# Row mean from eight more columns of a weight matrix, in place of products with a constant matrix

## The reference

```python
# layer "L2" in the names: language_ids picks a matrix per batch b
h = relu(einsum('bsh,bha->bsa', x, W1[ids]) + b1[ids])        # 256 features -> 64
adapted = einsum('bsa,bah->bsh', h, W2[ids]) + b2[ids]        # 64 -> 256
z = x + adapted
mean = jnp.mean(z, axis=-1, keepdims=True)
var = jnp.mean(jnp.square(z - mean), axis=-1, keepdims=True)
x = x + (z - mean) * rsqrt(var + 1e-5) * gamma + beta
# layer "L3"
x = x + einsum('bnh,boh->bno', x, W[subject]) + bias[subject]
```

## Time and profile before

| | |
|---|---|
| median of 3 runs | 1583.36 (1583.22 to 1584.35) |
| the profiled execution | 1581.01, span of its instructions 1579.2 |
| TensorE busy | 1570.2 of 1579.2 |
| VectorE, ScalarE, GpSimd busy | 1133.2, 931.4, 671.3 |
| granted TensorE clock | 0.9 or more of full speed in all 40 slices of the page |
| chain that ended last | TensorE 93%, GpSimd 3%, issue 2% |

### The profile page before, as it was taken

One profiled execution on the slowest core, in us unless ns is written; L12 is line 12 of the kernel. 1 busy time (PEld: TensorE's weight loads), 2 busy tenths in 40 slices (PEclk: granted clock), 3 DMA queues, 4 the chain that ended last, 5 costly groups with the idle time before them and its releaser, 6 DMA issues.

```text
span 1579.2 us, 22425 instructions
## 1 busy us (share of the span) xinstructions
PE 1570.2 (99%) x7916; PEld 1339.7 (85%) x7916; DVE 1133.2 (72%) x1685; ACT 931.4 (59%) x1683; POOL 671.3 (43%) x621
## 2 busy tenths in 40 slices
PE   9999999999999999999999999999999999999999
PEld 7888888999988888888888888888888888888898
DVE  6855556788889876777777776776776777657567
ACT  6655555666666665565666566656666666555444
POOL 7865544766787431432432442342342352038000
PEclk9999999999999999999999999999999999999999
DMA  4111105555520000010010010010010010022000
GB/s 161 56 53 54 54 27 179 169 183 177 171 83 31 20 34 27 14 41 27 15 40 28 14 41 27 14 40 28 14 41 27 14 41 27 15 59 77 14 14 28
DMA packets 31012, 85.98 MB, mean 54 GB/s; under 512 B 5030, under 2 KB 10534, under 8 KB 30774
## 3 DMA queue, kind: packets, MB, share of 16 engines
q1 hardware_dynamic: 30310, 83.21, 16.0%
q0 software_dynamic: 304, 1.10, 0.2%
q10 hardware_dynamic: 288, 0.26, 0.1%
HBM read 82.46 MB, written 2.10 MB: 54 GB/s over the span
## 4 chain that ended last, share of the span: by engine, by line
PE 93%; POOL 3%; issue 2%; DMA 0%; ACT 0%; DVE 0%; SPq 0%; POOLq 0%; ACTq 0%; DVEq 0%
PE up L682 13%; PE up L684 13%; PE up L683 13%; PE sum L441 12%; PE sum L442 12%; PE sum L443 12%; PE up L441 4%; PE up L442 3%; PE up L443 3%; PE up L450 2%; PE up L449 2%; PE up L451 2%; POOL expert_in L1496 1%; DMA raw<-in_shared 0%; POOL shared_up L1496 0%
## 5 line engine op out<-in xcount | busy, mean ns | idle before, releaser
L1305 ACT ACTIVATE hidden_hi<-up_tile 128x512 fp32r<-128x512 f32 x256 | 161.1, 629 | 189.2 <-DVE up_tile L2125 166.7
L2130 DVE TENSOR_TENSOR hidden_lo<-up_tile,hidden_hi 128x512 fp32r<-128x512 f32 x256 | 197.9, 792 | 44.7 <-ACT hidden_hi L1305 44.7
L2120 DVE TENSOR_TENSOR gate_tile<-up,gate_tile 128x512 f32<-128x512 f32 x192 | 130.1, 687 | 137.7 <-PE up L684 137.5
L441 PE MATMUL sum<-hidden_hi,down 128*128 128x512 f32 x512 | 199.2, 389 | 0.0
L443 PE MATMUL sum<-hidden_hi,down 128*128 128x512 f32 x512 | 199.2, 389 | 0.0
L442 PE MATMUL sum<-hidden_lo,down 128*128 128x512 f32 x512 | 199.2, 389 | 0.0
L683 PE MATMUL up<-x_sums,gate_up 128*128 128x512 f32 x512 | 199.2, 389 | 0.0
L682 PE MATMUL up<-x_sums,gate_up 128*128 128x512 f32 x512 | 199.2, 389 | 0.0
L684 PE MATMUL up<-x_sums,gate_up 128*128 128x512 f32 x512 | 199.2, 389 | 0.0
L2125 DVE TENSOR_TENSOR up_tile<-up_tile,gate_tile 128x512 f32<-128x512 f32 x192 | 184.0, 985 | 2.2
L1298 ACT ACTIVATE gate_tile<-gate_tile 128x512 f32<-128x512 f32 x192 | 119.9, 633 | 90.4 <-DVE gate_tile L2120 88.1
(11 more groups left out here) (332 smaller groups left out, 4004.9 us busy)
## 6 DMA issues: line engine op xcount, KB each, us to landing
raw<-in_experts SPq DMA_DIRECT2D x64, 512.0 KB, 3.3
raw<-in_l SPq DMA_DIRECT2D x51, 512.0 KB, 3.3
raw<-in_shared SPq DMA_DIRECT2D x23, 512.0 KB, 3.3
raw<-in_w SPq DMA_DIRECT2D x8, 256.0 KB, 2.6
x<-in_xT SPq DMA_DIRECT2D x3, 512.0 KB, 9.2
l_stage<-in_l SPq DMA_DIRECT2D x3, 512.0 KB, 4.2
out<-out_stage SPq DMA_DIRECT2D x6, 256.0 KB, 2.2
gate_w<-in_gw POOLq DMA_DIRECT2D x1, 1024.0 KB, 7.0
```

What stands on the lines that cost most here:

```text
L441: pe.matmul(out, wh, vh, start=start, stop=False)
L1305: A(hi[:, i], cu[:, i], ACT.Copy).then_inc(hi_done, 1)
L2120: V.tensor_tensor(t, ps, t, ALU.add).then_inc(c_done[m], 1)
L2130: V.tensor_tensor(lo[:, i], cu[:, i], hi[:, i].bitcast(f32), ALU.subtract).then_inc(lo_done, 1)
```

## The change

`minus_mean`, `x_row_sum` and its parts, `mean_stage`, `mean_part`, `row_sum` and `row_sum_hi` are dropped, and with them the stages `xs` and `mean`. The first matrix `l2_w1` becomes `w1m` with 72 columns for each batch and half: columns 64 to 71 hold -1/256 in the high part and 0 in the low part. So rows 64 to 71 of the first product are the negative row mean. A second tensor `v` goes into the second of the two `down` products: its rows 0 to 63 are the rounded ReLU (a third ReLU), rows 64 to 71 the mean rounded (a copy of 8 rows on ScalarE), rows 96 to 103 the rest of the mean (a subtraction of 8 rows on VectorE), and the others zero, written once after step 10. The matching rows of `w2[b][:, 1]`, in which the low part of the second matrix uses only rows 0 to 63 now, hold 1 in rows 64 and 96 and 0 elsewhere (`pick`, copied by ScalarE for each batch). `res` adds `x` itself. The fills of the eight columns stand in `center_b2` where that of `minus_mean` stood, and `l2_up_stage` of unit 0 waits for `b2_done`. The numbers in `WHEN` of the stages that stay are the same.

```diff
-STAGES = ["x2", "xs", "up", "mean", "within", "hid", "down", "res", "square", "scale", "var", "eps", "diag", "rstd",
+STAGES = ["x2", "up", "within", "hid", "down", "res", "square", "scale", "var", "eps", "diag", "rstd",
           "norm", "add", "x3", "x3l", "l3a", "outa", "l3b", "outb"]
...
+    w1m = place("l2_w1_mean", [P, B, 2, DT, A2 + MEAN_ROWS], f32r, over="shared_sums", skip=11264)
...
+    v = place("l2_mean_hidden", [2 * A2, BLK], f32r, over="raw", skip=12288)
...
                 pe.wait_ge(w_lo, PLAIN0 + L1_CH * NE1 + b0 + nb)
                 if i == 0:
                     pe.wait_ge(small_full, 16 * late_small)
+                    pe.wait_ge(b2_done, 1)
...
                     for dt in range(DT):
-                        m = slice(dt * A2, (dt + 1) * A2)
                         if b == b0:
                             pe.wait_ge(x2_lo, DT * i + dt + 1)
-                        last = product(unit_ps[i][0:A2, 0, c], w1r[:, b, 0, m], w1r[:, b, 1, m],
+                        last = product(unit_ps[i][0:A2 + MEAN_ROWS, 0, c], w1m[:, b, 0, dt], w1m[:, b, 1, dt],
                                        xh[:, dt, t], xl[:, dt, t], dt == 0, dt == DT - 1)
                 last.then_inc(l2_up, 1)
 
-            def mean_part(i, m):
-
-                b0, nb, t0, c0, n = unit(i)
-                out = unit_ps[i][:, m, c0:c0 + n]
-                for dt in range(DT):
-                    for part in (xh, xl):
-                        pe.matmul(out, minus_mean[:], part[:, dt, t0:t0 + n], start=dt == 0 and part is xh, stop=False,
-                                  skip_group_check=True)
-
...
+            def l2_down_stage(i):
+
+                b0, nb, t0, c0, n = unit(i)
                 if i in (1, 2):
                     pe.wait_ge(out_ready, 2 * i)
-                if "xs" in WHEN[i]:
-                    pe.wait_ge(xs_lo, i)
-                    pe.matmul(out, minus_mean[:], xsr[i // 2][:, 0, 0:n], start=True, stop=False)
-                    pe.matmul(out, minus_mean[:], xsr[i // 2][:, 1, 0:n], start=False, stop=True).then_inc(mean_done, 1)
-                    return
-                last = product_of_parts(out, t0, n)
-                last.then_inc(mean_done, 1)
-
-            def product_of_parts(out, t0, n):
-
-                for dt in range(DT):
-                    pe.matmul(out, minus_mean[:], xh[:, dt, t0:t0 + n], start=dt == 0, stop=False)
-                    last = pe.matmul(out, minus_mean[:], xl[:, dt, t0:t0 + n], start=False, stop=dt == DT - 1)
-                return last
-
-            def l2_down_stage(i):
-
-                b0, nb, t0, c0, n = unit(i)
                 if i == END:
                     pe.wait_ge(out_ready, 6)
-                    mean_part(i, 1)
                     x_part(i, 0)
                 pe.wait_ge(hid_relu, i + 1)
-                if i == END:
-                    mean_part(i, 0)
-                else:
-                    pe.wait_ge(x_centered, i + 1)
                 pe.wait_ge(l2_hid, i + 1)
                 for b in range(b0, b0 + nb):
                     c = slice(b % 2 * S, (b % 2 + 1) * S)
                     for m in range(DT):
                         out, k = unit_ps[i][:, m, c], slice(m * P, (m + 1) * P)
-                        pe.matmul(out, w2[b][:, 0, k], u[:, c], start=i != END, stop=False, skip_group_check=True)
-                        last = pe.matmul(out, w2[b][:, 1, k], u[:, c], start=False, stop=True, skip_group_check=True)
+                        pe.matmul(out, w2[b][:, 0, k], u[:, c], start=True, stop=False)
+                        last = pe.matmul(out, w2[b][:, 1, k], v[:, c], start=False, stop=True)
...
                 A(w3[b][:, 0], raw[:, s, 0:512], ACT.Copy)
-                A(w1r[:, b, 0], raw[:, s, 512:640], ACT.Copy)
+                A(w1m[:, b, 0, :, 0:A2], raw[:, s, 512:640].rearrange("p (t m) -> p t m", t=DT), ACT.Copy)
                 act.wait_ge(w2_centered, b + 1)
+                A(w2[b][A2:2 * A2, 1], pick[A2:2 * A2].to_broadcast([A2, D]), ACT.Copy)
                 A(w2[b][:, 0], raw[:, s, 640:896], ACT.Copy).then_inc(w_hi, 1)
...
                 if i == 0:
                     act.wait_ge(w_lo, PLAIN0 + L1_CH * NE1 + B)
+                    act.wait_ge(mean_rows, 1)
                 act.wait_ge(l2_up, i + 1)
                 if i:
                     act.wait_ge(l2_down, i)
                     act.wait_ge(l2_hid, i)
                 for b in range(b0, b0 + nb):
                     c = slice(b % 2 * S, (b % 2 + 1) * S)
-                    A(ru[:, c], unit_ps[i][0:A2, 0, c], ACT.Relu, bias=b1[:, b:b + 1])
-                    last = A(u[0:A2, c], unit_ps[i][0:A2, 0, c], ACT.Relu, bias=b1[:, b:b + 1])
-                last.then_inc(hid_relu, 1)
-
+                    for out in (ru, u, v):
+                        A(out[0:A2, c], unit_ps[i][0:A2, 0, c], ACT.Relu, bias=b1[:, b:b + 1])
+                c, m = slice(c0, c0 + n), slice(A2, A2 + MEAN_ROWS)
+                A(v[m, c], unit_ps[i][m, 0, c], ACT.Copy).then_inc(hid_relu, 1)
...
-                lo_part(w1r[:, b, 1], raw[:, s, 512:640], w1r[:, b, 0])
-                lo_part(w2[b][:, 1], raw[:, s, 640:896], w2[b][:, 0]).then_inc(w_lo, 1)
-
+                lo_part(w1m[:, b, 1, :, 0:A2], raw[:, s, 512:640].rearrange("p (t m) -> p t m", t=DT), w1m[:, b, 0, :, 0:A2])
+                lo_part(w2[b][0:A2, 1], raw[0:A2, s, 640:896], w2[b][0:A2, 0]).then_inc(w_lo, 1)
...
+                if b == 0:
+                    dve.wait_ge(ident_full, 16)
+                    V.tensor_tensor(pick[:], ident[:, A2:A2 + 1], ident[:, A2 + 32:A2 + 33], ALU.add)
...
             def center_b2():
 
-                V.tensor_scalar(minus_mean[:], ones[:], -1.0 / D, None, ALU.mult)
+                same = ones[:].rearrange("p (b t m) -> p b t m", b=B, t=DT)
+                for h, value in enumerate((-1.0 / D, 0.0)):
+                    V.tensor_scalar(w1m[:, :, h, :, A2:A2 + MEAN_ROWS], same, value, None, ALU.mult)
                 dve.wait_ge(b2_sum, 1)
                 linked(V.tensor_reduce(b2s[:], unit_ps[0][:, 1, 0:DT * B].rearrange("p (b t) -> p b t", t=DT), AX.X, ALU.add))
                 V.scalar_tensor_tensor(b2c[:], b2s[:].rearrange("p (b t) -> p b t", t=1).to_broadcast([P, B, DT]),
                                        -1.0 / D, cols[:, :, 0:DT], ALU.mult, ALU.add).then_inc(b2_done, 1)
 
+            def zero_rows():
+
+                dve.wait_ge(w_lo, PLAIN0 + L1_CH * NE1 + B)
+                V.tensor_scalar(v[A2:2 * A2], ones[A2:2 * A2, 0:1].to_broadcast([A2, BLK]), 0.0, None, ALU.mult).then_inc(mean_rows, 1)
+
...
-                if i != END:
-                    dve.wait_ge(mean_done, i + 1)
-                    if i:
-                        dve.wait_ge(x3_done, DT * i)
-                    for dt in range(DT):
-                        last = V.tensor_tensor(y[:, dt, c], x[:, dt, t0:t0 + n], unit_ps[i][:, 1, c], ALU.add)
-                    last.then_inc(x_centered, 1)
                 dve.wait_ge(hid_relu, i + 1)
-                V.tensor_tensor(u[A2:2 * A2, c], ru[:, c], u[0:A2, c].bitcast(f32), ALU.subtract).then_inc(l2_hid, 1)
+                V.tensor_tensor(u[A2:2 * A2, c], ru[:, c], u[0:A2, c].bitcast(f32), ALU.subtract)
+                m, r = slice(A2, A2 + MEAN_ROWS), slice(A2 + 32, A2 + 32 + MEAN_ROWS)
+                V.tensor_tensor(v[r, c], unit_ps[i][m, 0, c], v[m, c].bitcast(f32), ALU.subtract).then_inc(l2_hid, 1)
 
             def res_stage(i):
 
                 b0, nb, t0, c0, n = unit(i)
                 dve.wait_ge(l2_down, i + 1)
-                if i == END:
-                    dve.wait_ge(x3_done, DT * 3)
-                else:
-                    dve.wait_ge(x_centered, i + 1)
+                if i:
+                    dve.wait_ge(x3_done, DT * min(i, SUMMED))
                 for dt in range(DT):
                     for b in range(b0, b0 + nb):
                         c = slice(b % 2 * S, (b % 2 + 1) * S)
-                        xc = x[:, dt, b * S:(b + 1) * S] if i == END else y[:, dt, c]
                         last = V.scalar_tensor_tensor(y[:, dt, c], unit_ps[i][:, dt, c], b2c[:, b, dt:dt + 1],
-                                                      xc, ALU.add, ALU.add)
+                                                      x[:, dt, b * S:(b + 1) * S], ALU.add, ALU.add)
                     last.then_inc(centered, 1)
...
             hooks.setdefault(9, []).append(center_b2)
+            hooks.setdefault(10, []).append(zero_rows)
```

More of the change, by code:

```diff
@@ L21 @@
 FT = F // P
+MEAN_ROWS = 8
 NB = 4
@@ L49 @@
 RING = [0, 1, 2, 0]
-STAGES = ["x2", "xs", "up", "mean", "within", "hid", "down", "res", "square", "scale", "var", "eps", "diag", "rstd",
+STAGES = ["x2", "up", "within", "hid", "down", "res", "square", "scale", "var", "eps", "diag", "rstd",
           "norm", "add", "x3", "x3l", "l3a", "outa", "l3b", "outb"]
 WHEN = [dict(zip(STAGES, at)) for at in (
[4 rows of a table removed]
-for u in (0, 3):
-    del WHEN[u]["xs"]
[4 rows of a table added]
```

(31 more changed lines are left out.)

14 lines of the change are left out of this document (2 added, 12 removed), and 8 rows, old and new, of the table WHEN.

## The result

| | before | after |
|---|---|---|
| median | 1583.29 (1581.06 to 1584.35, 6 runs) | 1593.88 (1591.81 to 1595.78, 6 runs) |
| ratio after to before | | 1.0069, 95% interval 1.0059 to 1.0079 |
| profiled execution, span | 1581.01, 1579.2 | 1593.19, 1591.4 |

The change costs 10.6 us, not 5.85, and the time lies above the range. The page of after, part 1, as the earlier trace rows: TensorE issues twenty products fewer, and the span is 12 longer.

The account below looks back on a forecast made before the run. TensorE, busy 99% of the span, was taken as the bound. Unit costs 2.65 + 0.1 + 2.05 + 1.05 = 5.85, added to the profiled 1581.01, plus 2.35 to the median, gave 1589.2; range 1584.8 to 1591.0.

Parts of the forecast that it names:

- The `pick` copies of the earlier batches cost nothing: Late weight preparation before unit 0: ScalarE's added copies fall in its idle time, cost zero.
- three signs of being wrong: 8-row copy well under 0.37, VectorE less than 1 us late at unit 3's `x_lo`, or TensorE idle under 2 us.
- The gain on TensorE: Last phase: dropped products free 3.3 us together; 48 products widened to 72 columns add 0.3.
- A narrow instruction isn't a cheap one here: Hidden rows of each unit: 8-row copy costs 0.57 and subtraction 0.68 for 512 columns, 0.36 and 0.42 for 256.
- The rival: Hidden rows: 8-row copy and subtraction take 0.15 each, giving 1585.5; chance 0.08, and 0.04 with every wait covered, 1580.7.
- The fills: Before unit 0's first matrix: two fills on VectorE, 0.68 pitch then 0.25; 0.5 more if GpSimd is later too.
- Unit 0's mechanism: TensorE waits for `b2_done`, then for hidden rows behind the 8-row subtraction, then for squares; unit 0 costs 2.65.
- Unit 1: Second matrix starts about as before, the TensorE gain being eaten; cost 0.1 (0 to 0.3).
- Units 2 and 3: ScalarE and VectorE 1.56 late from unit 2, lasting to unit 3's `x_lo`; cost 2.05 (1.3 to 2.5).
- that rival: Units 2 and 3: the lag is absorbed within unit 2, total cost 3.1, time 1586.5; chance 0.17.
- The last unit: Third ReLU, copy and second subtraction delay its second matrix, in series to the last store; cost 1.05 (0.8 to 1.3).
- The clock: TensorE's waits lower its clock: three microseconds at half clock cost 1.5 more, 1590.7; chance 0.05, shared with another late queue.

Follow-up runs that it names:

- before_pick: The kernel before with one ScalarE copy added in each of the eight late weight splits, overwritten by GpSimd afterwards: median 1583.9, ratio 0.9999.
- prep_alone: The kernel before plus the change's weight preparation alone (strided first matrix, pick copies, VectorE's addition), GpSimd's low part still on 128 rows: median 1584.1, ratio 1.0003.
- full_split: The changed kernel with GpSimd's low part of the second matrix on all 128 rows again, pick copies still issued but overwritten: median 1590.6, ratio 1.0047.
- no_pick: The changed kernel without ScalarE's eight pick copies and with GpSimd's low part on all 128 rows again: median 1590.4, ratio 1.0038.
- early_pick: The changed kernel with the eight pick copies moved to steps 1 and 2 and without VectorE's pick addition: median 1592.7, ratio 1.0056.
- reorder: The changed kernel with the eight mean rows copied and subtracted first, then two ReLUs per batch, the third ones last: median 1589.5, ratio 1.0032.
- polite: The changed kernel with GpSimd waiting, before a batch's three subtractions, until VectorE has centred the next batch's second matrix: median 1590.3, ratio 1.0048.
- all_polite: The changed kernel with pick copies and fills moved early, mean rows first, and GpSimd waiting for VectorE's centring: median 1587.0, ratio 1.0020.
- all_three: The changed kernel with pick copies in steps 1 and 2, fills in step 1, and mean rows copied and subtracted first: median 1587.7, ratio 1.0023.

## Why the prediction was wrong

The direction was right, and so were most steps. The one that failed:

**"The `pick` copies of the earlier batches cost nothing: ScalarE idles in each of those steps until VectorE's gate product comes."** Taken as a sentence on ScalarE's copies it held: before_pick and prep_alone are at 0.9999 and 1.0003. What I took from it, that steps 3 to 9 stay as they are, didn't. I never costed the edit next to it, GpSimd's low part on 64 rows in place of 128, since it takes work away. It made `x_lo` 2.4 late (predicted 0.31; the copies' own part is the difference of full_split and no_pick, 0.6), and full_split, which changes this alone, brings 1590.6, 6.4 above before with its unit 0 at 2.45, where I had 5.85 and 2.65. The chain runs: 64 rows shift VectorE by 0.4; the centring then falls just behind GpSimd's start, where it can take 2.6 (and does twice in after); the gate product, `hidden_hi` and the next batch's preparation come late; so do `x_hi` and `x_lo` of unit 0, and the last of GpSimd's work with them; TensorE waits 3.1 and not 1.5; the clock falls. Of the 2.9 between after and full_split in unit 0, 1.9 is the lag (2.4 less 0.5). The other 1.0 I put down to the clock; no run isolates it. The one with this lag, the same order of the hidden rows and no fall is early_pick, whose unit 0 costs 4.1 and not 5.3, which fits.

The bare trace of before had the warning: in the steps 3 to 9 VectorE's centrings took 757 ns in the mean, where a lone one takes 0.42, and one of them 1.49. That one began 0.07 behind GpSimd, where 2.60 came out in after. An operation whose duration varies threefold between steps here held a wait inside it. None of my three signs of being wrong came up (the 8-row copy took 0.59, unit 3's `x_lo` was over 1 late, TensorE idled for over 2): they looked at the units, and the miss lay in steps 3 to 9.

Step by step:
- *The gain on TensorE.* Right: the pitch of 72 columns is 0.12 (1461.99, 1462.11), the wide pace I had taken.
- *"A narrow instruction isn't a cheap one here."* Right: 0.59 and 0.69 for 8 rows where I had 0.57 and 0.68; 0.42 for 256 columns. The rival is out.
- *The fills.* Right: the first took 0.74 beside GpSimd's last subtraction, the second, begun at 1461.09 behind GpSimd's end at 1461.07, 0.21 (forecast a pitch of 0.68, then 0.25). GpSimd was later too, but so were the fills, and the 0.5 more that I had for that case didn't come.
- *The zeroing of `v`.* 0.42 and not 0.68; it was off the path.
- *ScalarE per batch.* The late weights take it 1.57 for each batch, 1.04 before: 0.53 more, not 0.31 (the pick copy has a pitch of 0.42, the strided copy of the first matrix costs 0.1 more than the plain one).
- *Unit 0's mechanism.* Confirmed where the lag is absent: first product behind `b_centered`, second matrix behind the 8-row subtraction, 2.2 to 2.45 against 2.65.
- *Unit 1.* 0.2 against 0.1. *Units 2 and 3.* 2.3 against 2.05; the lag isn't absorbed, that rival is out too. My sign for unit 3 (first matrix 1.5 late behind `x_lo`) showed as a wait of 0.4 there and longer ones at the hidden rows.
- *The last unit.* 1.3 against 1.05; TensorE waits 1.94 for the subtraction. reorder takes nearly all of this and of units 2 and 3 away, which shows the cause.
- *The clock.* I gave it 0.05 together with any other late queue, and priced three microseconds at 1.5. It came, and together with the late queue: a chance of 0.05 was too small, since a late queue makes the waits that a fall can follow. The Trainium skill, "TensorE: Matmul & The Clock Gate", section "HAM oscillation", ties such falls to idle gaps between groups of products; the runs agree in part: the fall followed the waits of 3.1 in after and of 2.2 in polite, and there was none behind the 1.1 of full_split. But in all_polite it came behind waits of 1.2 and 1.0, all_three had waits of 1.2 and 0.9 at the same places and no fall, and the early fall at 309 us had no idle time before it.
- *The base.* I added to the median the 2.35 by which it stood above the profiled execution, and that was right in kind: the profile of before is one without the early fall of the clock.

## What to carry to other kernels

Where two engines hold each other up, as VectorE and GpSimd do here, cost every edit on either of them, those that shrink an instruction too: look for an operation whose duration varies from step to step, and at how far its start stands from the other engine's burst. A gap of a few tenths there was no slack here; a wait that fixed the order was worth more than it cost. And an undo run that restores two lines proves neither of them: undo them one by one.
